# Attention of a fused cross-attention and feed-forward kernel: head 1's mask and product on GpSimd in two steps, and the exponentials in the order 1, 0, 2, 3

## The reference

```python
Q = (x_text @ Wq).reshape(Bb, Tt, H, DH)
K = (x_vision @ Wk).reshape(Bb, Gg, H, DH)
scores = jnp.einsum('bthd,bghd->bhtg', Q, K) / np.sqrt(DH).astype(np.float32)
topv, topi = jax.lax.top_k(scores, K_TOP)          # K_TOP = 32
probs = jax.nn.softmax(topv, axis=-1)
attn = jnp.zeros_like(scores).at[bi, hi, ti, topi].set(probs)
attn_mean = attn.mean(axis=1)
c_t = jnp.einsum('btg,bgd->btd', attn_mean, x_vision @ Wv)
```

## Time and profile before

| What | Value |
| --- | --- |
| Median of 3 runs | 4450.14 us (4443.53 to 4450.18) |
| Profiled execution: its own time, its span | 4451.71 us, 4450.0 us |
| VectorE busy, share of the span | 3261.7 us, 73% |
| ScalarE busy | 2278.5 us, 51% |
| GpSimd busy | 1481.9 us, 33% |
| TensorE matrix products busy | 3424.6 us, 77% |
| Products `keep_top` (L410) | 128 of 3550 ns, 451.6 us |
| Exponentials (L532) | 128 of 2970 ns, 380.1 us |

### The profile page before, as it was taken

One profiled execution on the slowest core, in us unless ns is written; L12 is line 12 of the kernel. 1 busy time (PEld: TensorE's weight loads), 2 busy tenths in 40 slices (PEclk: granted clock), 3 DMA queues, 4 the chain that ended last, 5 costly groups with the idle time before them and its releaser, 6 DMA issues. The chain is left out here.

```text
span 4450.0 us, 56158 instructions
## 1 busy us (share of the span) xinstructions
PE 3424.6 (77%) x16934; PEld 2258.7 (51%) x16934; DVE 3261.7 (73%) x8951; ACT 2278.5 (51%) x2956; POOL 1481.9 (33%) x1287
## 2 busy tenths in 40 slices
PE   5575858888888888865775778649999999946776
PEld 3343535555555555532554555437777777722333
DVE  4398899989998999939788999723444444359996
ACT  1375758878877888832332333313333333337674
POOL 1022324433444443343454010011333333215564
PEclk8666777777777777777998899969999999977888
DMA  6200000000000000013220343343433333320111
GB/s 202 88 7 5 9 9 9 9 9 9 9 11 11 9 9 9 9 60 137 101 66 21 71 101 86 96 140 123 138 125 123 124 122 113 114 91 9 58 44 51
DMA packets 262469, 282.02 MB, mean 63 GB/s; under 512 B 60695, under 2 KB 183195, under 8 KB 261148
## 3 DMA queue, kind: packets, MB, share of 16 engines
q1 hardware_dynamic: 243146, 250.76, 18.3%
q10 hardware_dynamic: 15700, 15.42, 1.1%
q0 software_dynamic: 3328, 12.58, 0.7%
HBM read 213.68 MB, written 65.02 MB: 63 GB/s over the span
## 5 line engine op out<-in xcount | busy, mean ns | idle before, releaser
L643 PE MATMUL score<-KT,q 64*128 64x512 f32 (+1 forms) x1792 | 666.6, 519 | 287.8 <-ACT S L505 147.1
L405 DVE MAX8 cand<-S 128x8 f32<-128x100 f32 (+1 forms) x4096 | 680.6, 248 | 104.4 <-ACT S L505 66.2
L643 PEld LDWEIGHTS score<-KT,q 64*128 64x128 f32 x1792 | 429.4, 260 | 516.0 <-ACT S L505 266.0
L668 PE MATMUL up<-ctx,attnT 128*128 128x384 f32 (+1 forms) x1664 | 613.1, 517 | 0.0
L505 ACT ACTIVATE S<-score 128x1024 f32<-128x1024 f32 (+1 forms) x512 | 409.8, 832 | 124.7 <-PE score L643 124.6
L410 DVE SCALAR_TENSOR_TENSOR S<-S,tops,E 128x3202 f32<-128x3202 f32 x128 | 451.6, 3550 | 6.5 <-ACT E L532 6.5
L668 PEld LDWEIGHTS up<-ctx,attnT 128*128 128x128 f32 (+1 forms) x1664 | 324.2, 205 | 209.1 <-issue 53.8
L2090 DVE TENSOR_TENSOR ff_gelu<-ff_whole,ff_gelu 128x512 fp32r<-128x512 f32 x128 | 97.3, 760 | 429.8 <-ACT ff_gelu L2207 429.8
L514 ACT ACTIVATE E<-S,below 128x3202 bf16<-128x3202 f32 x128 | 379.6, 2965 | 28.1 <-issue 13.3
L532 ACT ACTIVATE E<-S,ebias 128x3202 f32<-128x3202 f32 x128 | 380.1, 2970 | 10.2 <-POOL ebias L362 9.9
L372 POOL TENSOR_TENSOR S<-S 128x512 f32<-128x512 f32 (+1 forms) x224 | 252.1, 1165 | 301.8 <-DVE S L410 301.5
(11 more groups left out here) (376 smaller groups left out, 6523.1 us busy)
## 6 DMA issues: line engine op xcount, KB each, us to landing
s_hankel<-scratch_K SPq DMA_DIRECT2D x128, 256.0 KB, 4.4
ff_w_low<-scratch_w1l SPq DMA_DIRECT2D x112, 256.0 KB, 2.6
ff_w_low<-scratch_w2l SPq DMA_DIRECT2D x112, 256.0 KB, 2.6
x_in<-in_x SPq DMA_DIRECT2D x8, 1024.0 KB, 6.8
scratch_xt<-xt_prep POOLq DMA_DIRECT2D x8, 1024.0 KB, 8.5
q<-scratch_qt SPq DMA_DIRECT2D x128, 64.0 KB
X<-in_L_ffn_w SPq DMA_DIRECT2D x2, 4096.0 KB, 21.2
mod_xt<-scratch_xt SPq DMA_DIRECT2D x32, 256.0 KB, 2.7
```

The source lines that it names most:

```text
L405: nc.vector.max(cand[:, h, 8 * k:8 * k + 8], S[:, b, h, k * SEG:end])
L643: last = nc.tensor.matmul(score[k % 2][:, j % 2, 0:w], lhsT=q[at, part, h // 2, :], rhs=KT[at, h // 2, chunk(j)], start=(part == 0), stop= ...
L668: last = nc.tensor.matmul(up[:, 0:DV], lhsT=attnT[0:w, e, c - 4 * g, :], rhs=ctx[0:w, c, :], start=(c == 0), stop=(c == GC - 1))
```

## The change

Head 1's product leaves VectorE. GpSimd does it in two instructions over all 3202 columns: a comparison of head 1's scores in `S` with the column of 32nd largest values, written back to `S` as 1 or 0, and a multiplication of that with the exponential in `E[:, 1, :]`. Both stand in GpSimd's list between the bias and the first sum, with a drain after each, and the comparison waits for the exponential of head 1. ScalarE forms the exponentials in the order 1, 0, 2, 3. Head 3's exponential, which writes to the same buffer as head 1's, now waits for GpSimd's multiplication (`first_kept`) instead of VectorE's product. `e_used` counts three products a tile instead of four, and the waits on it are renumbered. The first sum waits for head 0's product, the second for head 2's, its last three chunks for head 3's.

```diff
--- before.py
+++ after.py
@@ -316,9 +316,10 @@
         signs = E[:, 0, :].bitcast(BF16)[:, 0:G]
         s = {n: sem("attn_" + n) for n in (
             "ctx_in", "mask_in", "tmask_ready", "expected_set", "q_in", "score_done", "score_copied", "below_ready", "counted",
-            "flags_done", "tops_final", "lden_ready", "ebias_ready", "e_ready", "e_used", "summed01", "summed02", "summed", "turned",
+            "flags_done", "tops_final", "lden_ready", "ebias_ready", "e_ready", "e_used", "first_kept", "pool_passed", "summed01", "summed02", "summed", "turned",
             "turn_copied", "times_done", "u_copied", "u_stored", "passed")}
         ORDER = (1, 2, 3, 0)
+        KEPT = (1, 0, 2, 3)
         EARLY, LATE = (1, 2, 3), (0,)
         HALVES = -(-SCORE_CHUNKS // 2)
         GROUPS = H * HALVES
@@ -360,15 +361,21 @@
                 def turn(n, b):
                     pool.wait_ge(s["lden_ready"], n + 1)
                     nc.gpsimd.tensor_tensor(ebias[:, b, :], nmax[:], lden[:], ALU.subtract).then_inc(s["ebias_ready"], 1)
-                    pool.wait_ge(s["e_used"], H * n + 4)
+                    pool.wait_ge(s["e_ready"], H * n + 1)
+                    pool.sem_inc(s["pool_passed"], 1)
+                    nc.gpsimd.tensor_scalar(S[:, b, 1, :], S[:, b, 1, :], tops[:, b, 1, TOP - 1:TOP], None, ALU.is_ge)
+                    pool.drain()
+                    nc.gpsimd.tensor_tensor(S[:, b, 1, :], S[:, b, 1, :], E[:, 1, :], ALU.mult).then_inc(s["first_kept"], 1)
+                    pool.drain()
+                    pool.wait_ge(s["e_used"], (H - 1) * n + 3)
                     for j in range(SCORE_CHUNKS):
                         nc.gpsimd.tensor_tensor(S[:, b, 0, chunk(j)], S[:, b, 0, chunk(j)], S[:, b, 1, chunk(j)],
                                                 ALU.add).then_inc(s["summed01"], 1)
                     pool.drain()
-                    pool.wait_ge(s["e_used"], H * n + 5)
+                    pool.wait_ge(s["e_used"], (H - 1) * n + 4)
                     for j in range(SCORE_CHUNKS):
                         if j == 4:
-                            pool.wait_ge(s["e_used"], H * n + 6)
+                            pool.wait_ge(s["e_used"], (H - 1) * n + 5)
                         nc.gpsimd.tensor_tensor(S[:, b, 0, chunk(j)], S[:, b, 0, chunk(j)], S[:, b, 2, chunk(j)],
                                                 ALU.add).then_inc(s["summed02"], 1)
                     pool.drain()
@@ -406,7 +413,7 @@
 
                 def keep_top(n, b, h):
 
-                    dve.wait_ge(s["e_ready"], H * n + h + 1)
+                    dve.wait_ge(s["e_ready"], H * n + KEPT.index(h) + 1)
                     nc.vector.scalar_tensor_tensor(S[:, b, h, :], S[:, b, h, :], tops[:, b, h, TOP - 1:TOP], E[:, h % 2, :],
                                                    ALU.is_ge, ALU.mult).then_inc(s["e_used"], 1)
 
@@ -466,7 +473,6 @@
                     segments(n, b, 3)
                     if not first:
                         keep_top(n - 1, 1 - b, 0)
-                        keep_top(n - 1, 1 - b, 1)
                     thresholds(b, EARLY)
                     if not first:
                         keep_top(n - 1, 1 - b, 2)
@@ -484,7 +490,7 @@
                 turn(TILES - 2, 0)
                 turn(TILES - 1, 1)
                 check(TILES - 1, 1)
-                for h in range(H):
+                for h in KEPT[1:]:
                     keep_top(TILES - 1, 1, h)
 
             @block.scalar
@@ -509,7 +515,7 @@
                 def count_kept(n, b, h):
 
                     act.drain()
-                    act.wait_ge(s["e_used"], H * n + 1)
+                    act.wait_ge(s["e_used"], (H - 1) * n + 1)
                     act.wait_ge(s["below_ready"], 2 * n + (1 if h in EARLY else 2))
                     nc.scalar.activation(signs, S[:, b, h, :], ACT.Sign, bias=below[:, h:h + 1],
                                          accum_out=count[:, h:h + 1]).then_inc(s["counted"], 1)
@@ -526,9 +532,12 @@
                     nc.scalar.activation(lden[:], den[:], ACT.Ln, scale=float(H)).then_inc(s["lden_ready"], 1)
 
                 def probabilities(n, b, h):
-                    if h == 0:
+                    if h == KEPT[0]:
                         act.wait_ge(s["ebias_ready"], n + 1)
-                    act.wait_ge(s["e_used"], H * n + h + 1)
+                    if h == KEPT[3]:
+                        act.wait_ge(s["first_kept"], n + 1)
+                    else:
+                        act.wait_ge(s["e_used"], (H - 1) * n + {KEPT[0]: 2, KEPT[1]: 1, KEPT[2]: 3}[h])
                     nc.scalar.activation(E[:, h % 2, :], S[:, b, h, :], ACT.Exp, bias=ebias[:, b, h:h + 1],
                                          scale=SCALE).then_inc(s["e_ready"], 1)
 
@@ -571,11 +580,11 @@
                         copy_scores(n, b, 3, range(2, HALVES))
                     if old:
                         sums_of_exps(n - 1, 1 - b)
-                        probabilities(n - 1, 1 - b, 0)
+                        probabilities(n - 1, 1 - b, KEPT[0])
                     if older:
                         copy_turned(n - 2, b, 2)
                     if old:
-                        probabilities(n - 1, 1 - b, 1)
+                        probabilities(n - 1, 1 - b, KEPT[1])
                     if older:
                         copy_turned(n - 2, b, 3)
                     if new:
```

## The result

The changed kernel took 4703.6 us (median, 4699.8 to 4707.0) against 4446.8 for the kernel before on the same chip: a ratio of 1.0579, 95% interval 1.0561 to 1.0598, 257 us slower. Forecast were 4731 and slower. The profiled execution has a span of 4703.1 us, 253 more than before.

The account below looks back on a forecast made before the run. VectorE's work was taken to set the pace, with short waits for score copies. 29 x 8.8 = 255, 2 x 6.7 = 13 and 13 at the end gave +281 on the median of 4450.1: 4731, range 4590 to 4850.

Parts of the forecast that it names:

- Step 1: VectorE: one product of 3.5 us removed, 2.8 lost waiting for head 0's exponential, at best 0.7 a tile won.
- Step 2: GpSimd: the added comparison over 3202 elements, bounds 3.1 and 11.1 us, taken as 11.1.
- Step 3: GpSimd: the added multiplication of two 3202 tiles, taken as 7.8 us.
- Step 4: VectorE: head 0's product held by GpSimd's comparison until 2.7 us before its end, starting at 1014.0 instead of 1008.9.
- Rival C: GpSimd against VectorE: the block lasts the whole instruction, 84 us more, 4815 in all; chance 0.16.
- Step 5: Thresholds end at 1026.6; ScalarE's exponential of head 3 waits for the multiplication, 1025.4 instead of 1014.4.
- Step 6: GpSimd's sums, with products of heads 2 and 3 between chunks: the third ends at 1054.0, before 1044.3.
- Step 7: Back to the next tile through TensorE and ScalarE: first exponential at 1062.3, before 1052.81; 8.8 us a tile taken.
- its signs: Trace marks of a right forecast: head 0 product 7 to 9, period about 60, head 3's exponential idle 5 or more.
- Rival D: GpSimd finishes head 1 before ScalarE wants head 3's exponential, by about 1017: 22 us less, 4428; chance 0.04.
- Rival B: GpSimd's comparison takes only 3.1 us, at the rate of L1067; +5 a tile, 4605; chance 0.16.
- Rival E: The comparison is slow but nothing blocks; ScalarE's queue is late, about +7 a tile, 4667; chance 0.06.

Follow-up runs that it names:

- e1_chunked: The changed kernel with comparison and multiplication each split into seven chunks of 512 columns, all comparisons first; 4906.3 us.
- e7_product_first: The changed kernel with GpSimd waiting for head 0's product on VectorE before it starts the comparison; 4861.6 us.
- e5_read_beside: The kernel before with one added GpSimd comparison, reading 3072 columns of the context, its result needed by nothing; 4640.2 us.
- e6_write_beside: The kernel before with eight added GpSimd fills of a small integer tile, which read nothing; 4819.5 us.
- e9_in_place: The changed kernel with the exponentials of heads 2 and 3 written in place into S, their masks left out; 4704.1 us.
- e2_no_compare: The changed kernel without the comparison and its drain, so head 1's mask is left out; 4638.3 us.
- e3_order_only: The kernel before with exponentials and first two products in the order 1, 0, 2, 3, all products on VectorE; 4478.8 us.

## Why the prediction was right

- **Step 1** was exact: VectorE waits 2.81 us for head 0's exponential (2.8 forecast).
- **Step 2**, the comparison: 8.37 us, not 11.1. It was mis-sized by taking L1063's rate. The operation lies between the bounds, at 2.6 ns an element over 3202; on 512 columns, L1063's length, it takes 1.57 us in e1_chunked, 3.1 ns an element. So part of the error lies in carrying the rate of 512 columns over to 3202.
- **Step 3**, the multiplication: 6.9 us of work (6.92 where undisturbed in e7_product_first), not 7.8.
- **Step 4**, the hold: 4.8 us against 5.1, right by two errors that cancel. The release came 0.4 us before the comparison's end, not 2.7 (1060.89 - 3.53 = 1057.36, end 1057.78). So L1070's 2.7 does not carry over, and the Trainium skill's rule ("SBUF — State Buffer", which states in the section "SBUF: two separate sides" that the one which starts first has the shared pair of ports for its whole instruction; the section that the prediction names says this length only of VectorE's two-port modes) is here the better guide; e5_read_beside, released 1.9 before its end (1023.22 + 12.67 - 3.5 - 3.53 against 1030.80), lies between. That a GpSimd instruction which only writes does not contend with two SBUF inputs stands in the same page's section "Who interferes with whom", and e6_write_beside agrees: 7.00 us. Rival C had the condition nearly right and its price wrong: between the release and the comparison's end lay 0.4 us, not 2.7, and 4703.6 is far from its 4815.
- **Step 5**: head 3's exponential starts 21.6 us after the first one, forecast 22.8. Steps 2 and 3 were 3.6 too long, the release 2.3 too early.
- **Step 6**: the last sum ends at 49.9, forecast 51.4. Its pieces are right: 9.95 and 11.10 for the sums with one product in each, forecast 10.2 and 11.4.
- **Step 7**: T is 59.7, forecast 59.7, and that is luck: 1.5 less at the sums and as much more behind them. The wait that it walked back through, TensorE's for the second sum's fourth chunk, is the one that e9_in_place shows; the chunk ends at 40.1, forecast 41.5, and 19.6 follow, forecast 18.2. The increase is 8.1 a tile, not 8.8: the step's own lower bound, by which the mean tile's extra 1.4 before goes into the waits. 31 intervals gave 245, forecast 268; the end 11, forecast 13.
- What the prediction did not see: it walked one way back to the next tile, while there are two, through ScalarE's waits (58.0 or more a tile by e2_no_compare) and through the sums (59.7). It also put the order at nothing beyond VectorE's wait; e3_order_only shows 35 us where nothing else is changed. In the changed kernel head 2's exponential waits 7.0 us and is hidden behind head 3's wait, as step 5 says.
- Of its signs, the product's length (8.3) and the period came. Head 3's exponential idles 2.5 us on the multiplication, not 5 or more, as head 2's before it took 7.0. GpSimd's busy time rose by 782 us, not 608, and VectorE's rose by 137 and did not fall: the products of heads 2 and 3, in between the chunks of the sums, lengthen the sums and are held themselves.
- Rival D needed GpSimd to be done by about 1017, 14.4 after the first exponential; it took 21.6. Rival B fell with the comparison's 8.37. Rival E fell with the hold.

## What to carry over

Idle time on an engine is worth only what fits between the waits around it: ask which instruction, by its end, lets the next round begin, and what may stand before it. An instruction moved to GpSimd that reads memory held up VectorE's products, which have two inputs, to 0.2 to 1.9 us before its end, so the place beside them is not free: in e5_read_beside it cost 193 us. And where removing one cause gives little or nothing, remove two: two rings of nearly the same length hide each other.

## What the runs showed of the hardware

- A comparison with a column over 3202 f32 elements takes 8.37 us on GpSimd (2.6 ns an element), over 512 1.57 us (e1_chunked), to 8-bit integers over 3072 7.94 us; the rate depends on the operation.
- A held-up instruction is released before the holder's end: 0.2 us before for the multiplication in e2_no_compare, 0.4 for the comparison in place, 1.9 for the comparison into another tile, 2.7 in the earlier trace rows. Each of the first three is the same in all 32 tiles to 0.02 us. What sets this is open.
- The hold is not only for instructions with two inputs: `margin` (L449 after, three columns, one tile read) takes 0.50 us beside a chunk of the changed kernel's first sum, 0.17 before. This was not tested.
- Filling 3202 bytes a partition on GpSimd takes some 2.9 us (22.98/8, with a drain after each).
- A sum's chunk of 512 takes 1.09 or 1.27 us with the same operation, by the distance of its operands.
